# The first four tiles in FP16, and the four loaded tiles of two halves at places 12 to 15 of 20

## The reference

```python
x = x + tanh(g_xattn[0]) * attention(ctx_1024, ctx_1024, layernorm(x), ...)
n = layernorm(x)
logits = n @ gate_w.T                       # 1024 x 8
topk_probs, topk_idx = top_k(softmax(logits), 2)
h = gelu(n @ w1[:, e, :].T + b1[e])         # 512 wide, for the two experts e of each token
y = h @ w2[:, e, :].T + b2[e]
x = x + tanh(g_ffn[0]) * sum over the two of (y * topk_probs)
```

## Time and profile before

| | us |
|---|---|
| median of 3 runs | 103.31 (103.09 to 103.7) |
| the profiled execution's own time | 103.78 |
| its span | 102.0 |
| mean granted TensorE clock | 0.922 of full speed |
| PE busy / PEld busy | 86.3 / 70.5 |
| DVE / ACT / POOL busy | 63.0 / 58.3 / 51.3 |

### The profile page before, as it was taken

How to read it: one execution, slowest core, us unless ns; L and a number is a source line. 1 busy time by engine, 2 the same in 40 slices (tenths; PEclk the granted TensorE clock), 3 DMA queues, 4 the chain that set the end, 5 groups by cost and what they waited for, 6 DMA issues and landing times.

```text
span 102.0 us, 3022 instructions
## 1 busy us (share of the span) xinstructions
PE 86.3 (85%) x925; PEld 70.5 (69%) x925; DVE 63.0 (62%) x275; ACT 58.3 (57%) x193; POOL 51.3 (50%) x91
## 2 busy tenths in 40 slices
PE   5949888878996689999997789899999999999500
PEld 1445555743653459989986579778999999999500
DVE  2377759999888948996531202375468885527380
ACT  5356799849668811547666356956666574741000
POOL 6975698308777776740000000373577777700480
PEclk9999999999999855569999958999999999999995
DMA  2999996910111453860222245420110011128315
GB/s 36 328 420 431 431 431 241 289 42 26 55 52 52 124 140 107 249 246 13 58 38 45 52 103 124 90 71 18 40 34 18 26 42 58 46 53 278 113 55 151
DMA packets 11839, 13.32 MB, mean 131 GB/s; under 512 B 1475, under 2 KB 10327, under 8 KB 11568
## 3 DMA queue, kind: packets, MB, share of 16 engines
q1 hardware_dynamic: 10112, 10.59, 31.7%
q0 software_dynamic: 1024, 1.92, 5.8%
q10 hardware_dynamic: 688, 0.61, 2.2%
HBM read 9.03 MB, written 4.29 MB: 131 GB/s over the span
## 4 chain that ended last, share of the span: by engine, by line
PE 29%; POOL 20%; DMA 15%; issue 14%; DVE 12%; SPq 6%; POOLq 1%; ACT 1%; DVEq 0%
POOL dispatched L417 13%; PE bank L927 12%; DMA res<-results 5%; PE bank L900 5%; PE bank L902 4%; DMA x_sb<-in_x 4%; SPq L394 3%; PE bank L901 3%; SPq L396 3%; DMA dispatched<-rows,slot 3%; DMA results<-y_sb,in_rows 2%; POOL results L510 2%; PE bank L879 2%; DMA in_rows<-dispatched 2%; POOL rstd L454 2%
## 5 line engine op out<-in xcount | busy, mean ns | idle before, releaser
L666 ACT ACTIVATE hid<-bank,wp 128x64 f32<-128x64 f32 (+1 forms) x112 | 28.0, 339 | 19.8 <-PE bank L902 12.4
L510 POOL DMA_INDIRECT results<-y_sb,in_rows x16 | 16.2, 1013 | 27.1 <-ACT y_sb L620 23.4
L927 PE MATMUL bank<-w_sb,hid 128*128 (+2 forms) x192 | 23.3, 299 | 0.0
L417 POOL DMA_INDIRECT dispatched<-rows,slot x16 | 16.5, 1032 | 9.1 <-issue 8.2
L927 PEld LDWEIGHTS bank<-w_sb,hid 128*64 128x64 f32 (+1 forms) x192 | 19.9, 178 | 0.2
L900 PE MATMUL bank<-xs_t,w_hi 128*128 128x128 f16 (+1 forms) x80 | 13.9, 215 | 1.3 <-DVE xs_t L1260 1.3
L901 PE MATMUL bank<-xs_t,w_hi 128*128 128x128 f16 (+1 forms) x80 | 13.8, 213 | 0.0
L902 PE MATMUL bank<-xs_t,w_lo 128*128 128x128 f16 (+1 forms) x80 | 13.8, 212 | 0.0
L1260 DVE COPY xs_t<-bank 128x256 f16<-128x256 f16 x16 | 4.6, 290 | 14.2 <-PE bank L879 14.2
L688 PE MATMUL bank<-ones 128*128 128x512 bf16 x38 | 11.6, 423 | 1.2 <-DVE ones L995 1.2
L897 PE MATMUL bank<-xs_f,w_sb 128*128 128x64 f32 x64 | 9.7, 315 | 0.0
(11 more groups left out here) (198 smaller groups left out, 171.0 us busy)
## 6 DMA issues: line engine op xcount, KB each, us to landing
w_sb<-in_w SPq DMA_DIRECT2D x2, 2048.0 KB, 10.7
results<-zeros SPq DMA_DIRECT2D x1, 1024.0 KB, 5.7
w_second<-in_w SPq DMA_DIRECT2D x4, 256.0 KB, 4.3
res<-results SPq DMA_DIRECT2D x4, 256.0 KB, 5.0
in_rows<-dispatched SPq DMA_DIRECT2D x12, 65.0 KB, 2.0
dispatched<-pad_rows SPq DMA_DIRECT2D x9, 65.0 KB, 2.4
in_rows<-dispatched SPq DMA_DIRECT2D x16, 32.5 KB, 2.1
ctx_sb<-in_ctx_t SPq DMA_DIRECT2D x1, 512.0 KB, 4.9
```

The lines of the kernel that those rows point to most:

```text
L417: pool.indirect_dma_start(rows_dram, bass.IndirectOffsetOnAxis(ap=slot[:, t, k:k + 1], axis=0), rows[:, t, k, :], None).then_inc(sent, 16)
L510: pool.indirect_dma_start(results_dram, bass.IndirectOffsetOnAxis(ap=in_rows[:].bitcast(U32)[:, t, TARGET:TARGET + 1], axis=0), y_sb[:, t, ...
L666: mm = act.activation(hid[:, t % HIDS, b, part], hid_ps[h % len(hid_ps)][:, at + part.start:at + part.stop], ACT.Gelu_apprx_tanh, bias=b1[ ...
L927: mm = pe.matmul(to[part, :], hid[:, t % HIDS, b, part], weights, start=False, stop=b == BLOCKS - 1)
```

## The change

It has these parts:

- Tiles 0 to 3 take FP16 weights like the others: `gather` writes the high and the low part into two halves of its bank, ScalarE copies both into `xs_first`, and `hidden` makes three FP16 products. `w1_hi` is made in eight parts, six of them before the gelu table is loaded, and `w1_lo` in pairs between the one-hots of the tiles, since hidden(t) now waits for the first 2t + 2 of its eight parts.
- The four tiles of two halves are tiles 12 to 15. Tiles 4 to 11 and 16 to 19 are whole.
- SyncE loads tiles 4 to 7 first, one load each, then the rows of tiles 0 to 3 (needed for gates and targets only) in two loads instead of eight, then tiles 8 to 19. There are 22 loads instead of 28. ScalarE gates tile 0 after the gelu of tile 6 instead of 5, and so on.
- VectorE makes the gates and the last slots before the table, and the table after the one-hots of tile 1; TensorE waits for the table before output(1), and for `sel` alone before output(0). Tile 6 is split after the copies of tiles 4 and 5.
- The small arrays of the table stay integers or become FP16, with eight fewer POOL instructions; two counts are reduced in one instruction. `keep_clock` after the last ranks has 6 matmuls instead of 3.

VectorE, after the count of tiles of the last group: first before, then after (`slot` holds the row numbers that the last sends wait for, `lane` and `sel` serve the bias).

The diff, cut to its core:

```diff
-SHARED = EARLY + MIXED
-WHOLE = N_TILES - SHARED
+MIXED_AT = 12
+MIXED_TILES = range(MIXED_AT, MIXED_AT + MIXED)
+WHOLE = N_TILES - EARLY - MIXED
-IN_FP32 = 4
-LAG = 2
+LAG, LATER = 2, 2
+FIRST_LOADS = 4
-    W1_HIGH: [14.9],
+    W1_HIGH: [14.9, 14.91, 22.2, 23.6, 28.0, 33.0],
-              (RANKS, 2): 2, (X1_T, 3): 3, (ROUTE, 3): 6, (RANKS, 3): 3}
+              (RANKS, 2): 2, (X1_T, 3): 3, (ROUTE, 3): 6, (RANKS, 3): 6}
-HIGH_PARTS = 4
+HIGH_PARTS = 8
...
-            return [...2 * t + i...] if t < SHARED else [(slice(0, SLOT_TILE), EXPERTS + t)]
+            if t < EARLY:
+                first = 2 * t
+            else:
+                first = EXPERTS + t - EARLY + max(0, min(t - MIXED_AT, MIXED))
+            if t < EARLY or t in MIXED_TILES:
+                return [(slice(i * PART, (i + 1) * PART), first + i) for i in range(2)]
+            return [(slice(0, SLOT_TILE), first)]
...
-            for t in range(EARLY, SHARED):
-                load_shared(t)
-                load_shared(t - EARLY)
-            for t in range(SHARED, N_TILES):
-                sp.dma_start(in_rows[:, t, :], ...)
+            regions = rows_dram[FIRST_ROW:PAD_ROW, :].rearrange("(t i r) w -> i r t w", i=2, r=REGION)
+            for t in range(EARLY, N_TILES):
+                if t == EARLY + FIRST_LOADS:
+                    for i in range(2):
+                        sp.dma_start(in_rows[i * PART:(i + 1) * PART, 0:EARLY, :], regions[i, 0:PART, :, :]).then_inc(loaded_first, 16)
+                for part, i in entries(t):
+                    sp.dma_start(in_rows[part, t, :], rows_dram[bass.ds(first[i - EXPERTS], part.stop - part.start), :]).then_inc(loaded[t], 16)
...
-            pool.tensor_copy(slot_no[:], slot_i[:]).then_inc(numbers_set, 1)
...
-                act.activation(xs_f[:, t, :], gather_ps[t % 2][:, 0:P], ACT.Copy).then_inc(first_ok, 1)
+                act.activation(xs_first[:, t, :, :], gather_ps[t % 2][:, 0:2 * P].rearrange(...), ACT.Copy).then_inc(first_ok, 1)
...
-                if t in (1, 2):
-                    weights_hi(w1_hi, w1_sb, ld_w1, w1hi_ok, t + 1)
+                if t == 1:
+                    weights_hi(w1_hi, w1_sb, ld_w1, w1hi_ok, 7)
-                if EARLY + 1 <= t < 2 * EARLY + 1:
-                    first_gated(t - EARLY - 1)
+                if EARLY + LATER <= t < 2 * EARLY + LATER:
+                    first_gated(t - EARLY - LATER)
...
-                            mm = pe.matmul(gather_ps[i % 2][:, 0:P], rows_16[:, t, c, :], hot[:, i, t, :, :],
+                            mm = pe.matmul(gather_ps[i % 2][:, c * P:(c + 1) * P], rows_16[:, t, c, :], hot[:, i, t, :, :],
...
                     pe.wait_ge(first_ok, t + 1)
+                    pe.wait_ge(w1_ok, 2 * t + 2)
...
-                        if t < IN_FP32:
-                            mm = pe.matmul(to, w1_sb[:, e, f], xs_f[:, t, part], start=True, stop=True)
+                        pe.matmul(to, w1_hi[:, e, f], xs[:, 0, part], start=True, stop=False)
+                        pe.matmul(to, w1_hi[:, e, f], xs[:, 1, part], start=False, stop=False)
+                        mm = pe.matmul(to, w1_lo[:, e, f], xs[:, 0, part], start=False, stop=True)
...
-                    pe.wait_ge(ld_w1, 16)
                     pe.wait_ge(ld_w2, 16)
+                    pe.wait_ge(sel_ok, 1)
+                if t == 2:
                     pe.wait_ge(table_ok, 3)
...
-            for i in range(1, EARLY):
-                for k in range(len(HOT_CHUNKS)):
-                    one_hots(i, k)
-            for i in range(PARTS):
-                low_weights(i)
+            for i in range(EARLY):
+                if i:
+                    for k in range(len(HOT_CHUNKS)):
+                        one_hots(i, k)
+                if i == 1:
+                    table(lane_made)
+                for e in range(2 * i, 2 * i + 2):
+                    low_weights(e)
...
-            for t in range(EARLY, EARLY + LAG + 1):
-                if t >= IN_FP32:
-                    split_rows(t)
+            for t in range(EARLY, EARLY + LAG):
+                split_rows(t)
             for t in range(EARLY, EARLY + LAG):
                 copy_rows(t)
+            split_rows(EARLY + LAG)
```

More of the change, by code:

```diff
@@ L149, in gated_block @@
         slot_i = sb("slot_i", [P, EXPERTS, PART], I32)
[L150 to L153, removed]
+        edge_i = sb("edge_i", [P, 2, EDGES], I32)
         place_i = sb("place_i", [P, FURTHER], I32)
[L155 to L161, removed]
+        past_i = sb("past_i", [P, 2, SEGMENTS], I32)
+        after = sb("after", [P, 2, SEGMENTS], F16)
+        same = sb("same", [P, 2, SEGMENTS], F16)
+        seg_wrap = sb("seg_wrap", [P, 1], I32)
+        seg_expert = sb("seg_expert", [P, 1], I32)
         seg_first = sb("seg_first", [P, 1], F32)
         seg_row = sb("seg_row", [P, 1], F32)
-        seg_less = sb("seg_less", [P, 1], F32)
+        seg_less = sb("seg_less", [P, 1], F16)
         x_sb = sb("x_sb", [P, TILES, P], F32)
@@ L376, in _ @@
             sp.wait_ge(table_ok, 3)
-            for u in range(0, 2 * MIXED, LOADS):
+            at_mixed = MIXED_AT - EARLY
+            for u in range(at_mixed, at_mixed + 2 * MIXED, LOADS):
                 of = table_values(sp, tile_experts, EXPERTS - 1, u)
                 for i in range(1, LOADS, 2):
-                    k = (u + i) // 2
+                    k = (u - at_mixed + i) // 2
                     sp.dma_start(w2_second[:, k, :], w2[:, bass.ds(of[i], 1), :]).then_inc(ld_second[k], 16)
@@ L666, in _ @@
                         mm = act.activation(hid[:, t % HIDS, b, part], hid_ps[h % len(hid_ps)][:, at + part.start:at + part.stop], ACT.Gelu_apprx_tanh,
-                                            bias=b1[:, experts[i], b:b + 1], scale=1.0 if t < IN_FP32 else 1.0 / WSCALE)
+                                            bias=b1[:, experts[i], b:b + 1], scale=1.0 / WSCALE)
                     if b % HALVES == HALVES - 1:
@@ L922, in output @@
                     for part, i in entries(t):
-                        if EARLY <= t < SHARED and part.start:
-                            weights = w2_second[:, t - EARLY, f]
+                        if t in MIXED_TILES and part.start:
+                            weights = w2_second[:, t - MIXED_AT, f]
                         else:
@@ L1039, in lanes @@
                 v.wait_ge(dve, n)
[L1040 removed]
+                v.tensor_scalar(sel[:, 0:EXPERTS], iota_i[:], lane[:, 0:1], 1.0 / WSCALE, ALU.is_equal, ALU.mult).then_inc(sel_ok, 1)
                 return n
@@ L1181, in table @@
                 v.wait_ge(found_ps, 1)
-                n = then(v.scalar_tensor_tensor(tile_row[:], found(0)[0:1, :], float(PAD_ROW // PART), place_no[0:1, :], ALU.add, ALU.add))
+                n = then(v.scalar_tensor_tensor(tile_row[:], found(0)[0:1, :], float(PAD_ROW // PART), place_i[0:1, :], ALU.add, ALU.add))
                 v.tensor_scalar(tile_experts[:], found(1)[0:1, :], float(EXPERTS), float(EXPERTS - 1), ALU.add, ALU.min).then_inc(table_ok, 1)
@@ L1194, in fill_rows_of @@
                     count_tiles()
-                    lane_made = lanes()
                     one_hots(0, 0)
+                    gates(g)
+                    slots(g)
                     locate()
@@ L1201, in fill_rows_of @@
                     one_hots(0, 2)
-                    table(lane_made)
-                    gates(g)
-                    slots(g)
                 else:
```

143 lines of the change are left out of this document (60 added, 83 removed).

## The result

The changed kernel takes 98.76 us (median of 4 runs, 97.88 to 99.24), the kernel before, run beside it, 103.5 (103.09 to 104.22). The ratio is 0.9588, with a 95% interval of 0.9528 to 0.9647: 4.7 us faster. Some executions of each kernel here are longer, at a lower granted clock, and the measured ratios leave these out. I had predicted 96.5 with a range of 94.2 to 99.6. The direction and the range hold; the size was 2.3 us too good, and one step behind it was wrong in a way that the sum hid.

What follows compares the result with a forecast made beforehand. GpSimd's sends and scatters at the ends, TensorE between, were taken to bound the kernel. 51.7 + 26.25 + 3.2 + 0.05 + 13.98 = 95.2 of span, 6.8 less; 103.31 - 6.8 = 96.5 us, range 94.2 to 99.6.

Steps and rivals of the forecast that it cites:

- Part 1 and 2: Up to tile 4: VectorE's work puts hidden(0) at 39.0; tiles 0 to 3 in FP16 let tile 4 start at 51.7.
- (c): Rival, TensorE before tile 4: the clock stays at 1.2 GHz until then; time 100.7; chance 0.08.
- (b): Rival, tiles 0 to 3: short matmuls pay for issue, 1.88 per 24, period 3.9; time 99.8; chance 0.07.
- the row of eight: TensorE: eight matmuls of 24 columns took 0.35, some 0.026 each, used to price the 24 FP16 matmuls.
- Part 3: Data for tile 4: sends, loads, split, turn and copy done at 50.4, hidden below TensorE's 51.7.
- the sends land at 45.8: GpSimd's sends to experts: the last lands 0.65 earlier, since its slots no longer wait behind the table.
- T4: TensorE's start of tile 4, its first matmul: 56.64 in the kernel before, predicted at 51.7.
- no low clock after 46: Sign, TensorE: once the high clock returns near 44, no low clock after 46.
- Rival (e): Tile 4's load 2 us late by collision with second weights: T4 52.4, time 97.2; chance 0.60 together with the forecast.
- (d): Rival, whole tiles 4 to 11: low clock lasts on, 1.43 more each, slower than before, up to 112; chance 0.03.
- Part 4: T4 to the last scatter: 26.25 to tile 16, 3.2 to tile 15's result, GpSimd's 0.9 of waiting gone.
- Moving the mixed tiles thus gains almost nothing on TensorE by itself: TensorE from T4 to tile 16: 26.25 against 27.49 with a low-clock spell; the place gives an earlier first load.

Runs made afterwards that it cites:

- 5: Changed kernel, with VectorE waiting, before the low weights of experts 2 and 3, for a GpSimd memset behind its last send: 97.02 us, 0.935 of the kernel before.
- 11: Changed kernel with VectorE's wait for the last send, second experts' weights loaded before tile 12's load, and 5 and 6 added clock-keeping matmuls: 95.34 us, 0.9177 of before.
- 12: Kernel of 11 with VectorE's wait one step later, behind the one-hots of tile 2: 95.83 us, 0.9255 of the kernel before.
- experiment 1: Changed kernel with the second experts' W2 loads issued behind the loads of tiles 4 to 7 and the early tiles: 101.94 us, 0.982 of the kernel before.
- 10: Kernel of 5 (VectorE's wait) with the four tiles of two halves back at places 4 to 7: 101.09 us, 0.9773 of the kernel before.
- 2: Changed kernel with the four tiles of two halves back at places 4 to 7: 104.63 us, 1.0105 of the kernel before.
- 9: Kernel before, with only VectorE's order changed: tiles 4 and 5 split and copied back before tile 6 is split: 102.4 us, 0.9933 of before.
- 3: Changed kernel with 12 added GpSimd memsets in front of its first send: 99.26 us, 0.9503 of the kernel before.
- 4: Changed kernel with 3 clock-keeping matmuls after the last ranks instead of 6: 98.37 us, 0.9509 of the kernel before.
- 6: Changed kernel with GpSimd's small memset behind its last send, VectorE not waiting for it: 98.07 us (one run).
- 7: Changed kernel with VectorE making all one-hots first, then the low weights of experts 2 to 7: 99.68 us, 0.961 of the kernel before.
- 8: Changed kernel with the slot numbers that the one-hots compare converted to FP32 by GpSimd: 99.77 us (one run).

## Why the prediction was right, and where it was not

**Part 1 and 2 hold.** Said: 39.0, 0.75, hidden(1) at 43.9, a period of 3.1, hidden(3) ending at 50.85. Measured: 39.26, 0.70, 43.60, 49.51 - 43.60 = 5.91 for two periods, and 50.22. The INT32 one-hots cost nothing (0.67 for 512 columns, 0.68 before); the clock came back at 43.5, near the 44 that I expected, but fell only at 40, about 1 us later than said. So hidden(0) still ran at 2.4 GHz, where the sum had 1.35 at the low clock; that gain hid the later start. Rivals (b) and (c) are out: 24 matmuls in 0.70 start 0.029 apart. (The 0.026 that I took from the row of eight is also the spacing of their starts: the row's 0.35 includes the end of the last.) The Trainium skill ("TensorE: Matmul & The Clock Gate", "Wait — 56ns, not 53.3ns?") gives some 62 ns per matmul with hardware decode off, and a floor of about 25 ns between starts with either decode path; the 29 ns here lie near the floor.

**Part 3 failed.** The step "the sends land at 45.8" is where: the last one landed at 49.17. I had priced the sends by their order and their usual 0.96, and never asked what VectorE does while GpSimd carries one out. Where the last send was not held to the end of VectorE's row, T4 was 50.5 to 51.1 (5, 11 and 12), a little earlier than the 51.7 that I had for TensorE's own work. Here T4 was 52.59, just outside the 50.4 to 52.5 that I had named. Behind TensorE's wait of 1.36 came the second low stretch, against my "no low clock after 46"; without the wait, in 5, 11 and 12, there is none. Rival (e) named the late load and nearly the right T4 (52.4), but for a collision that experiment 1 rules out. What (d) feared, a low clock among the whole tiles, did come, but for 3.4 us only.

**Part 4: right sums, wrong account.** T4 to tile 16 took 26.81 instead of 26.25; with no low clock (5) it is 25.52, so the gaps at tiles 4 to 7 (1.0) were set too high: with whole tiles there one wait of 0.2 is left of them. Mixed tiles cost 79.40 - 69.06 = 10.34, not 10.7. The result of tile 15 came 82.20 + 0.34 - 79.40 = 3.14 behind tile 16 (3.2), VectorE released the last scatter as said, and the tail was 13.18 instead of 13.98. But "Moving the mixed tiles thus gains almost nothing on TensorE by itself" is wrong: 10 shows 2.3 us from T4 to tile 16 at full clock, and 2 shows 6.9 us of span in all, or 5.4 us of time by the ratios. I had the scatters' schedule in hand and used it only for the new place.

**The sum.** 52.59 + 26.81 + 3.14 + 0.28 + 13.18 = 96.0 of span, against 95.2 predicted. That it came so near is in part luck: T4 was 0.9 late, T4 to tile 16 and the wait for the last scatter 0.8 longer than said, and a tail 0.8 shorter, which nothing in the prediction foresaw, gave half of that back. The other 1.4 us of the miss is in the step from one execution to the median: I put the median 0.47 under the profiled execution; here it lies 0.88 above. The four runs differ in granted clock (0.924 to 0.958), and with 0.97 to 1.00 (11) four runs agree within 0.7 us. Inferred from this, not shown run by run: most of that spread is the length of the low stretches. Of the gain itself, 2 shows that none is left without the new place, and 9 shows 0.7 for the order of the splits; no run undoes the FP16 weights of tiles 0 to 3 alone, so their own share stays open.

## What to carry to other kernels

Where the chain of waits names a transfer that GpSimd starts, look first at how long GpSimd took to issue it, and at what VectorE did meanwhile: a wait of 1.2 us put into VectorE gave back 1.7 us of the median and 2.9 of the fastest run. Price an instruction order on one engine by what it closes to another, not only by its own length. And a part that "gains nothing by itself" should be priced by undoing it alone, down to the last engine of the tail.

## What the runs showed of the hardware

In eight traces without a timely pause (the change, 1 to 4, 6 to 8) the last send ended 0.84 or 0.85 us behind the end of a gapless row of VectorE instructions with two inputs in SBUF, and in 12 behind the stop put there. The send of 1.66 us at 36.00 in the kernel before fits too: a row that ends at 36.41 + 0.41 = 36.82, and 0.84 more is 37.66. The Trainium skill ("SBUF — State Buffer", "Who interferes with whom") says that a VectorE instruction with two SBUF inputs contends with a GpSimd instruction that reads SBUF, and that the order of issue decides which of them is blocked. The trace agrees that VectorE holds the send (6.92 us, and 0.96 with VectorE standing still), and shows that a whole row of instructions can do so, not one only. The same section reports a probe in which `tensor_tensor` did not stall DMA; here a send was held for 6.91 under a row that begins with six one-hots, which are such instructions (7).

What neither explains is when a send inside such a row is held to its end. In the kernel before, sends at 41.14, 42.44 and 43.71, begun well inside such a row (39.94 to 47.46), took 0.99, 0.97 and 0.96. The sends held for 6 us began 0.15 to 0.5 us behind the row's start. But the place in the row does not decide it either: in the change the send at 38.22 began 0.40 behind the start of low weights at 37.82, which one-hots follow without a gap up to 40.44, and took 1.12.

```profile
37.82 1.29 DVE L1198 SCALAR_TENSOR_TENSOR w_lo<-w_sb,w_hi 128x512 f16<-128x512 f32 x2
```

```profile
38.22 1.12 POOL L412 DMA_INDIRECT dispatched<-rows,slot  x1 [0.30 <-issue]
```

It ended 0.83 behind the end of the first of these two low weights (37.82 + 0.69 = 38.51), so it was held by one instruction at most, and not by the row. What tells the two cases apart stays open.
